# The way from the last coupling of a two-layer kernel to its routed expert groups: sums, whole downs and input parts placed anew, with four shared jobs ahead of the groups

## What is computed

```python
head, wrist, proprio = context_c[:, :42], context_c[:, 42:84], context_c[:, 84:]
full_agg = context_c.mean(axis=1)
hp_agg = jnp.concatenate([head, proprio], axis=1).mean(axis=1)
wp_agg = jnp.concatenate([wrist, proprio], axis=1).mean(axis=1)
gate_logits = jnp.concatenate([full_agg, hp_agg, wp_agg], axis=-1) @ gate_w + gate_b
...
gate_scores = softmax(gate_logits * (1.0 + scale) + shift)
topk_w, topk_i = top_k(gate_scores, 2)
...
for e in range(4):
    h = gelu(context_c @ ew1[e] + eb1[e])
    y = h @ ew2[e] + eb2[e]
    out = out + w_be[:, e] * mask[e] * y
shared = gelu(context_c @ sw1 + sb1) @ sw2 + sb2
return out + shared
```

## Time and profile before

| | before |
|---|---|
| median of 3 runs, us | 982.37 (981.58 to 983.87) |
| profiled execution, us | 980.21 |
| its span, us | 978.7 |
| busy TensorE, VectorE, ScalarE, GpSimd, us | 931.9, 805.7, 815.4, 549.7 |
| granted TensorE clock, mean | 0.989 |
| last coupling matmul of TensorE to first group matmul, us from the span's start | about 499 to 543.56 |

### The profile page before, as it was taken

One profiled execution on the slowest core, in us unless ns is written; L12 is line 12 of the kernel. 1 busy time (PEld: TensorE's weight loads), 2 busy tenths in 40 slices (PEclk: granted clock), 3 DMA queues, 4 the chain that ended last, 5 costly groups with the idle time before them and its releaser, 6 DMA issues. The chain is left out here.

```text
span 978.7 us, 25964 instructions
## 1 busy us (share of the span) xinstructions
PE 931.9 (95%) x8653; PEld 745.9 (76%) x8653; DVE 805.7 (82%) x3572; ACT 815.4 (83%) x2174; POOL 549.7 (56%) x677
## 2 busy tenths in 40 slices
PE   8999999999999999999978899999999999999887
PEld 7899989898989899853236688886877777776566
DVE  6766989889898989899997466766888988996985
ACT  6998889898989898867786699997788888886886
POOL 4345646364646555525935147666788888891051
PEclk9999999999999999999998899999999999999899
DMA  9100000000000000000243888821100000000003
GB/s 375 54 2 2 2 2 2 2 2 2 1 2 2 2 2 2 2 1 22 108 133 104 273 300 286 281 88 30 26 22 15 24 24 23 24 2 2 1 1 87
DMA packets 35796, 57.19 MB, mean 58 GB/s; under 512 B 3536, under 2 KB 26832, under 8 KB 35280
## 3 DMA queue, kind: packets, MB, share of 16 engines
q1 hardware_dynamic: 35664, 55.53, 17.0%
HBM read 40.31 MB, written 11.01 MB: 52 GB/s over the span
## 5 line engine op out<-in xcount | busy, mean ns | idle before, releaser
L270 PE MATMUL PB<-RR_s 128*128 128x256 f32 (+1 forms) x468 | 155.7, 333 | 9.2 <-DMA RR_s<-XD 4.2
L409 ACT ACTIVATE W<-W,small 128x128 f32<-128x128 f32 x384 | 149.0, 392 | 11.9 <-DVE small L400 11.1
L421 POOL TENSOR_TENSOR W<-W,small 128x512 f32<-128x512 f32 x96 | 100.6, 1053 | 100.3 <-DVE small L415 100.3
L271 PE MATMUL PB<-RR_s 128*128 128x256 f32 (+1 forms) x468 | 142.2, 304 | 0.0
L272 PE MATMUL PB<-RR_s 128*128 128x256 f32 (+1 forms) x468 | 142.1, 304 | 0.0
L2070 POOL TENSOR_TENSOR AR_s<-AR_s,small 128x512 f32<-128x512 f32 x128 | 129.7, 1042 | 15.9 <-DVE small L2063 15.9
L1379 DVE TENSOR_TENSOR RR_s<-AR_s,RR_s 128x512 fp32r<-128x512 f32 x108 | 81.0, 755 | 54.4 <-ACT RR_s L1370 54.3
L2063 DVE CUSTOM_DVE_ANT_0 AR_s<-PB,W 128x128 f32<-128x128 f32 x512 | 111.0, 286 | 2.7 <-PE PB L2054 1.0
L270 PEld LDWEIGHTS PB<-RR_s 128*128 128x128 f32 x468 | 89.2, 191 | 25.7 <-issue 14.2
L400 DVE CUSTOM_DVE_ANT_0 W<-PB,W 128x128 f32<-128x128 f32 x384 | 86.0, 283 | 13.4 <-PE PB L390 12.7
L349 DVE COPY AR_s<-PB 128x512 f32<-128x512 f32 x128 | 84.9, 684 | 13.6 <-PE PB L272 13.0
(11 more groups left out here) (446 smaller groups left out, 2653.7 us busy)
## 6 DMA issues: line engine op xcount, KB each, us to landing
RR_s<-W1D SPq DMA_DIRECT2D x13, 512.0 KB, 4.1
RR_s<-XD SPq DMA_DIRECT2D x52, 128.0 KB, 2.9
RR_s<-W2D SPq DMA_DIRECT2D x13, 512.0 KB, 4.4
W<-in_w SPq DMA_DIRECT2D x1, 5881.5 KB, 24.6
XD<-RR_s SPq DMA_DIRECT2D x18, 256.0 KB, 3.3
HQ<-W1D SPq DMA_DIRECT2D x6, 512.0 KB, 4.1
HQ<-XD SPq DMA_DIRECT2D x24, 128.0 KB, 2.9
HQ<-W2D SPq DMA_DIRECT2D x6, 512.0 KB, 4.5
```

The costliest lines, as they stand in the source:

```text
L270: nc.tensor.matmul(out, lh, rh, start=True, stop=False)
L271: nc.tensor.matmul(out, ll, rh, start=False, stop=False)
L409: e = nc.scalar.activation(SS[r][:, hl], SS[r][:, hl], ACTF.Exp, bias=mx[r][:, h:h + 1], scale=-1.0, accum_out=rc[r][:, h:h + 1])
L421: nc.gpsimd.tensor_tensor(s3, s3, over(rc[r], 2, [128, 4, 128]), ALU.mult).then_inc(s_nrm, 1)
```

## The change

- The last pair's coupling on VectorE is done in one go right behind the pair before it; the sums of chunks 2 to 7 stand behind all coupling, each of two reductions (the first gives head and wrist at once) and not three.
- The gate's weights are scaled and added up once at GpSimd's start (gate3), so that TensorE multiplies the raw sums; GpSimd's five operations on the sums are gone.
- NF is 4. The four shared jobs ahead (WHOLE) have single-precision downs: ScalarE's gelu goes to one of eight whole buffers, no high and low part are made, and a down is four matmuls of single-precision weights and input. In these turns all four up steps come first, then all four down steps of the job before; the gating's matmuls stand at other places.
- All low parts of the inputs are GpSimd's, ahead of pool_gating; the parts of chunks 5 to 7 have places of their own in the first buffers of the groups' weights and inputs, so no part and no store waits for a buffer. ScalarE makes parts 0 to 3 ahead of the last tanh and 4 to 7 ahead of the gelus of jobs 1 and 2. The split weights are staged in another order for this.
- Chunks 5 to 7 are read back from XD (sp_again) for their shared jobs behind the groups, of which there are now four.
- The groups' bias arithmetic moves from GpSimd to VectorE, behind the tables. The clearing of HF for the groups' sums stands behind pool_gating and covers four chunks, not three.
- Query and key of the next attention come one turn earlier (NJ - 2).

The diff, cut to its core:

```diff
@@
-        hs, ws, psm, agg = sm(32), sm(32), sm(32), sm(96)
+        sums = sm(96)
+        hs, ws, psm = [sums[:, 32 * i:32 * i + 32] for i in range(3)]
+        gate3, gate_scaled = sm(12), sm(12)
...
@@ dve_agg
-            for dst, a, b in ((hs, 0, 42), (ws, 42, 84), (psm, 84, 128)):
-                t = nc.vector.tensor_reduce(dst[:, 4 * c:4 * c + 4], xb[:, :, a:b], AX.X, ALU.add)
-            t.then_inc(s_ag, 1)
+            nc.vector.tensor_reduce(sums[:, 0:64].rearrange("p (m b) -> p b m", m=2)[:, 4 * c:4 * c + 4, :],
+                                    xb[:, :, 0:84].rearrange("p b (m t) -> p b m t", m=2), AX.X, ALU.add)
+            nc.vector.tensor_reduce(psm[:, 4 * c:4 * c + 4], xb[:, :, 84:128], AX.X, ALU.add).then_inc(s_ag, 1)
...
-        STAGE = WG1 + WG2 + XG + [XP[3], XP[4]]
+        EARLY = [XP[3], XP[4], WG1[1], WG2[1], XG[1]]
+        STAGE = EARLY + [WG1[0], WG2[0], XG[0]]
+        PART = [XP[i] for i in range(5)] + EARLY[2:]
...
-        NF, NG, RING = 5, 19, 3
+        NF, NG, RING, WHOLE = 4, 19, 3, 4
...
@@ sp_part
-            if c >= 2:
-                sp.wait_ge(sem, stored(c - 2))
...
+        def sp_again(c):
+            sp.wait_ge(s_up, 4 * (c - KEPT) + 4)
+            nc.sync.dma_start(XP[c - KEPT].rearrange("p (s r) -> p s r", s=4).bitcast(F32), XD[c * 512:c * 512 + 512, :].rearrange("(s p) r -> p s r", s=4)).then_inc(s_we, 16)
...
@@ act_up
+            if n < WHOLE:
+                if n < 2:
+                    act.wait_ge(s_x2, 4 * n + 2 * (k // 2) + 2)
+                else:
+                    act.wait_ge(s_dn, g - 7)
+                act.wait_ge(s_up, g + 1)
+                nc.scalar.activation(whole(g), PB[k][:, :], ACTF.Gelu_apprx_tanh, bias=b1).then_inc(s_ge, 1)
+                return
...
@@ pe_down
+            if n < WHOLE:
+                if k == 0:
+                    if n < 2:
+                        pe_after_couple(p)
+                    pe.wait_ge(s_ty, n - 1)
+                pe.wait_ge(s_ge, 4 * n + k + 1)
+                nc.tensor.matmul(PB[p][:, :], w("sw2")[:, columns(k)], whole(4 * n + k), start=k == 0, stop=k == 3).then_inc(s_dn, 1)
+                return
...
-        AHEAD = {(NJ - 1, 0): 0, (NJ - 1, 1): 1}
-        GATING_MM = {(2, 0): 1, (3, 0): 2, (3, 3): 3, (4, 1): 4}
-        GATING = {(2, 0): 1, (2, 3): 2, (3, 2): 3, (4, 0): 4}
-        PARTS = {1: (2, 3), 2: (4, 5), 3: (6, 7)}
+        AHEAD = {(NJ - 2, 0): 0, (NJ - 2, 1): 1}
+        GATING_MM = {(1, "down"): 1, (2, "up"): 2, (2, "down"): 3, (3, "down"): 4}
+        PARTS = {1: (4, 5), 2: (6, 7)}
...
@@ pe_layers
+            for n in range(WHOLE + 1):
+                for k in range(4):
+                    pe_up(n, k)
+                if (n, "up") in GATING_MM:
+                    pe_gating(GATING_MM[(n, "up")])
+                if n:
+                    for k in range(4):
+                        pe_down(n - 1, k)
+                if (n, "down") in GATING_MM:
+                    pe_gating(GATING_MM[(n, "down")])
...
@@ dve_layers
+            for p in range(1, 4):
+                for s in range(2):
+                    dve_agg(p, s)
+            dve_gating(1)
+            dve_down(0, 3)
+            dve_gating(2)
+            dve_gating(3)
+            for n in range(1, WHOLE - 1):
+                dve_down(n, 3)
+            dve_gating(4)
...
@@ pool_layers
-            pool_part(1)
+            for c in range(CH):
+                pool_part(c)
+            pool_gating()
             pool.wait_ge(s_x2, 8)
             nc.gpsimd.memset(HF[:, NF * 512:N], 0.0).then_inc(s_hz, 1)
-            pool_gating()
```

More of the change, by code:

```diff
@@ L1438, in pe_gating @@
                 pe.wait_ge(s_gte, 7)
+                pe.wait_ge(s_ag, 8)
                 for j in range(3):
-                    mm = nc.tensor.matmul(PB[6][0:32, 0:4], agg[:, 32 * j:32 * j + 32], w("gatew", 128, 4 * j, 4 * j + 4), start=j == 0, stop=j == 2)
+                    mm = nc.tensor.matmul(PB[6][0:32, 0:4], sums[:, 32 * j:32 * j + 32], gate3[:, 4 * j:4 * j + 4], start=j == 0, stop=j == 2)
                 mm.then_inc(s_gtm, 1)
@@ L1567, in dve_gating @@
                 v.tensor_copy(by_group, PB[7][:, 76:152]).then_inc(s_gt, 1)
+                eb4 = bias_by.rearrange("p (e k g) -> p e k g", e=4, k=5)
+                dve.wait_ge(s_gt, 24)
+                for e in range(4):
+                    b = v.tensor_tensor(eb4[:, e], over(w("eb", 128, 5 * e, 5 * e + 5), 2, [128, 5, 19]), over(by_group[:, 19 * e:19 * e + 19], 1, [128, 5, 19]), ALU.mult)
+                b.then_inc(s_gt, 1)
+                dve.wait_ge(s_gt, 25)
+                v.tensor_tensor(bias_by[:, 0:190], bias_by[:, 0:190], bias_by[:, 190:380], ALU.add).then_inc(s_gt, 1)
+                dve.wait_ge(s_gt, 26)
+                v.tensor_tensor(group_bias, bias_by[:, 0:95], bias_by[:, 95:190], ALU.add).then_inc(s_gt, 1)
             if i == 4:
@@ L1682, in pe_layers @@
                     pe_couple(p, y, st)
-            for n in range(NJ + 1):
+            for n in range(WHOLE + 1):
[8 more added lines that the diff above has]
+                    pe_gating(GATING_MM[(n, "down")])
+            for n in range(WHOLE + 1, NJ + 1):
                 for k in range(4):
@@ L1744, in act_layers @@
             for t in range(7, 19):
+                if t == 16:
+                    act_part(0)
                 if t == 17:
-                    act_part(0)
-                    act_part(1)
+                    for c in range(1, 4):
+                        act_part(c)
                 for p, y, st in turn_steps(t):
@@ L1794, in dve_layers @@
                     for p_, y, st in turn_steps(t):
-                        if p_ == p and (p, y, st) != (3, 2, 4):
+                        if p_ == p:
                             dve_couple(p, y, st)
-            for n in range(NJ + 1):
-                for c in PARTS.get(n, ()):
-                    dve_part(c)
+            for p in range(1, 4):
[8 more added lines that the diff above has]
+            dve_gating(4)
+            for n in range(WHOLE, NJ + 1):
                 for k in range(4):
@@ L1804, in dve_layers @@
                         dve_up(n, k)
[L1805 to L1809 removed]
+                    if 4 * n + k < 4 * NJ - 1:
                         dve_down(n - 1, k)
[L1811 to L1812 removed]
         def pool_layers():
@@ L1867, in sp_layers @@
             sp_second(NG - 1)
+            for c in range(KEPT, CH):
+                sp_again(c)
             sp.wait_ge(s_qz, 2)
```

124 lines of the change are left out of this document (42 added, 82 removed).

## The result

| | before | after |
|---|---|---|
| median, us | 981.98 (980.75 to 983.87, 4 runs) | 966.16 (964.96 to 967.18, 4 runs) |
| ratio, 95% interval | | 0.9837 [0.9816, 0.9857] |
| profiled execution's span, us | 978.7 | 965.4 |
| granted clock, mean | 0.989 | 0.996 |
| first group matmul, us | 543.56 | 524.96 |

The change makes the kernel 15.8 us faster. A later measurement of the same two kernels gives 967.01 against 981.93, 0.9838 [0.9822, 0.9853].

What follows compares the result with a forecast made beforehand. A chain of latencies was taken to precede a TensorE-bound loop. Turn 5 starting 12.7 us earlier, 2.2 of lower clock and a 0.59 wait were put together at 15.4 us, giving a 967.0 us median; range 963.5 to 972.0.

Steps and rivals of the forecast that it cites:

- 2: up of job 1: TensorE's walk: a third input part on ScalarE delays the first gelu by 0.3 us; up of job 1 starts at 502.8.
- 4: a chunk's sums; gate matmuls: VectorE's six chunk sums at 0.65 us each end at 508.8; gate matmuls run right behind job 0's down, at 509.1.
- 5: VectorE's eleven operations done: Gating under up 2 and down 1: VectorE's eleven operations done at 511.6, second gating matmuls 512.6, tables 517.7 instead of 534.57.
- Step 3: Whole down on TensorE: four single-precision matmuls of 0.90 us instead of twelve, 3.6 us against 2.7; job 0's ends at 509.1.
- dearer downs: Rival, chance 0.08: single-precision matmuls in the downs take 1.18 us each, 4.5 us on top, giving 971.5.
- Step 7: First group's input: load 0.8 us behind the tables, at 518.5; first matmul 5.64 us later, at 524.1, as TensorE arrives.
- late data: Rival, chance 0.17: the 3.35 us from tables to first load are SyncE's own; 969.6, or 971.8 with a falling clock.
- Step 8: After up 4 and down 3, TensorE waits 0.5 us for group 0's second weights; turn 5 in effect at 530.9.
- Step 6: Up 3, down 2, last gating matmul to 524.1; GpSimd's 11.5-us chain ends by 523.1, hidden; VectorE's bias arithmetic costs nothing.
- The lower clock: At the groups' start 12 matmuls regain full clock, 2.2 us; by another reading these stay lost, giving 969.2.
- Nothing gained: Rival, chance 0.03: SyncE's loads, not TensorE, bind the group loop, so an earlier start is lost; 982.
- slower: Rival, chance 0.04: the granted clock stays at its lower level through TensorE's walk; 14.7 us lost, 997.

Runs made afterwards that it cites:

- e10: The changed kernel measured again, unchanged, over more rounds and with a second profile: 967.01 us, ratio 0.9838 to before.
- e12: The changed kernel with twelve more transposes of the same tile filling TensorE's 1.92-us wait in the attention: 965.29 us, ratio 0.9833 to before.
- e2: The changed kernel with four more matmuls in job 0's whole down, ahead of the gate matmuls: 970.89 us, ratio 0.9887 to before.
- e6: The kernel before with only the sums' edit: gate weights scaled once, raw sums multiplied, five GpSimd operations gone: 978.02 us, ratio 0.9957 to before.
- e1: The changed kernel with GpSimd's five operations put back between the sums and the gate matmuls: 971.66 us, ratio 0.9894 to before.
- e11: The changed kernel with job 3's down ahead of job 4's up and each group's second weights behind its own input: 964.64 us, ratio 0.9822 to before.
- e5: The changed kernel with the four jobs ahead having downs in parts (twelve matmuls, VectorE's low parts): 975.78 us, ratio 0.993 to before.
- e4: The changed kernel with five shared jobs ahead, all with whole downs, and three behind the groups: 973.64 us, ratio 0.9914 to before.
- e8: The changed kernel with five whole-down shared jobs ahead and the next attention's query and key in the last turn again: 966.72 us, ratio 0.9842 to before.
- e7: The changed kernel with job 3's down ahead of job 4's up and group 0's second weights ahead of group 1's input: 965.35 us, ratio 0.9833 to before.
- e3: The changed kernel with input parts 5 to 7 sharing the buffers of parts 0 to 2 again, no reloads: 967.22 us, ratio 0.9848 to before.

## Why the prediction was right, step by step

The prediction was 967.0 with 963.5 to 972.0; measured were 966.16 and 967.01. Its way of 15.4 us is 15.1 by the first pair of profiles, 15.5 to 16.0 by the mean of the two of before (184.67) less 169.19, 168.80 and 168.68 (after, e10, e12). The forecast for the profiled execution, 964.8, was missed by 1.9 us (966.68), by the fall of the clock in the attention; that the median is met within 0.9 us is in part luck, as the prediction had no term for what such falls do to either median.

| step | predicted | measured in after |
|---|---|---|
| 2: up of job 1 | 502.8 | 502.47 |
| 3: a single-precision matmul | 0.90 us | 0.88 (four in 3.52, 505.32 to 508.84) |
| 4: a chunk's sums; gate matmuls | 0.65; 509.1 | 0.65; 508.84 |
| 5: VectorE's eleven operations done | 511.6 | 511.85 |
| 5: second gating, tables | 512.6, 517.7 | 512.18, 517.46 |
| 6: last gating matmul done | 524.1 | 524.08 |
| 6: GpSimd's chain done, beneath down 2 | by 523.1 | 519.85 |
| 7: first group load | 518.5 | 518.23 |
| 7: load to first matmul | 5.64 us | 6.73 (5.99 in e10; 5.78 in e12, where TensorE did not wait) |
| 8: turn 5 in effect | 530.9 | 531.2 |

- *Step 3 and dearer downs.* The pair of rows from the attention in the earlier trace rows, 0.86 apart, was the right neighbour: 0.88, and 0.86 for the four that e2 added with the same weights. The rival's 1.18 is refuted.
- *Step 7 and late data.* The 3.35 us between tables and first load in the kernel before were not SyncE's own: now they are 0.77. The rival is refuted. In e6, where the stores still end late, it is 2.6. What was off is the other half, load to matmul: taken as one number from one execution, it is 6.7 in after and 6.0 in e10. In the first profile that made the wait of 0.88.
- *Step 8.* The wait of 0.5 us for group 0's second weights didn't come in after (in e2 and e1 there is one of 0.3 and 0.5); the mistake and the one in step 7 have opposite signs, so turn 5 is met within 0.3 us by two errors, not by none.
- *Step 6.* GpSimd's gating chain took 7.9 us (511.95 to 519.85), not 11.5, chiefly because its wait of 2.83 us for VectorE (ahead of 529.79 before) is gone. It was hidden either way, so the number didn't count. The bias arithmetic on VectorE, bounded at 1 to 3.9 us, took 2.3 (517.64 to 519.97), also hidden.
- *The lower clock.* The 2.2 us at the groups' start came back as counted, granted clock 1.00 over the walk; the reading by which they would stay lost is refuted for this stretch. What the prediction lacked is the other place: it said that no idle stretch of that length was left ahead of the groups and looked no further, though a 1.9-us wait of the attention is enough in some executions. That, not the walk, is why the first pair of profiles shows 13.3 us between spans.
- *Nothing gained* and *slower*: the walk and the loop ran at full clock. Turns 5 to 7 of after have no wait of 0.3 us or more; e10 and e12 have one in turn 6, and e11 has one ahead of turn 8. So the loads nearly bind in the first turns, which is a small part of what *nothing gained* feared; from turn 8 up to the query a turn is 5.5 to 5.6 us in all of them.
- *A slip.* The 27.2 us of work (120 matmuls) set against the 44.3 us up to 543.56 count the down of job 4, which runs in turn 5: it is 108 matmuls, 24.5 us. Nothing in the sum rests on it.
- *What no step had:* without a fall the rest is 285.1 to 285.2 in e10, e11 and e12, 284.8 in both profiles of before. These 0.3 us were not looked into.

## What to carry to other kernels

- Walk the engine that will bound the stretch, instruction by instruction, each with its price from a row, and let every other engine's chain only show that it ends earlier; here TensorE's steps up to the data wait were met within 0.5 us each. Where a data wait ends the walk, take its price from more than one execution, and look at the next turns too: the loads behind it may be as late.
- A dearer matmul can be the cheaper one: four whole downs cost TensorE 3.1 us more, and with their low parts out of VectorE's queue they still brought 6.9 us net (e5).
- When the number of jobs ahead changes, look at what is placed by counting from the end (e4 against e8: 6.4 us).

## What the runs showed of the hardware

- *The clock after short waits.* Behind the same wait of 1.92 or 1.93 us in the attention the granted clock is at 1.2 GHz for some 3 us in six profiles and stays at 2.4 in seven; the same kernel has both (after, e10). Near the start it fell behind waits of 1.96, 1.98 and 2.34 us (e6, e10, e8) and did not behind 1.94, 2.08, 2.23, 2.45 and 2.77 us (e7, e5, e11, e12, e3). Waits of 0.6 to 0.95 us in the walk were never followed by it; those of 2.26, 2.52, 3.19, 4.32 and 5.49 us in the walk and at the groups' end (e5, e6, e1, e4, before) each were. Near the end, where the code is the same in all, it falls in every one of the fourteen profiles though no wait there is longer than 1.5 us: between the matmul behind a wait of 1.5 us and the one behind the next wait, of 1.1 to 1.2 us. TensorE of after, and its window:

```profile
897.46 0.66 PE L2579 MATMUL PB<-W,HFXT 128*128 128x128 f32 x4 [1.47 <-DVE AR_s L2535]
...
901.33 1.12 PE L2610 MATMUL PB<-W,AR_s 128*128 128x128 f32 x4 [1.20 <-DVE AR_s L2535]
```

```profile
901.20:904.50 3.30, 3.17 (x21) 2.50 (x22) 2.34 (x17) 2.90 (x9) 0.00 (x0) 0.50 0.00 0
```

  So the length of one wait does not tell whether a fall follows.
- *A small VectorE operation behind a GpSimd one.* L1511, 32x4 elements with both inputs in SBUF, took 1.06 us in after and ended at 510.61; it took 1.04 to 1.06 in the six other profiles (e4, e7, e8, e10, e11, e12) in which GpSimd is at an input part just then. It takes 0.15 us in the seven others, before, e1, e2 and e3 among them, where GpSimd is idle at that moment. GpSimd's timeline of after has two input parts that end at 510.60:

```profile
508.09 2.51 POOL L1287 TENSOR_TENSOR RR_s<-XF,RR_s 128x512 fp32r<-128x512 f32 x2 [0.83 <-ACT RR_s L1283]
```

  The Trainium skill (SBUF — State Buffer, SBUF: two separate sides) says that a GpSimd operation and a VectorE one with two SBUF inputs take a pair of ports as an exclusive lock, for the whole instruction. The trace agrees for this operation: blocked until 0.01 us behind the part's end. It doesn't for every one: GpSimd's L1470 reads SBUF too and stands in after's trace for 1.04 us (GpSimd's recorded times are rough), and a VectorE operation with two SBUF inputs ran inside that time in 0.16 us.

```profile
512.33 1.04 POOL L1470 TENSOR_TENSOR small<-small 32x4 f32<-32x4 f32 x1
...
512.92 0.16 DVE L1532 TENSOR_TENSOR HFXT<-HFXT,W 32x16 f32<-32x16 f32 x1
```

  Here the 0.9 us are hidden beneath up 2; with TensorE closer behind it, they would not be.
